# Cross-attention with a routed expert layer: eight expert tiles started from an early table

## The reference, cut to what matters

```
x = x + attention(context, context, layernorm(x))      # K, V from 120 context rows, one head, 8 batches
logits = layernorm(x) @ Wg + bg ; e = argmax(logits)   # one of 8 experts per row
h = gelu(layernorm(x) @ W1[e] + b1[e])
x = x + h @ W2[e] + b2[e]
```

## Time and profile before

| what | value |
|---|---|
| median of three runs | 483.49 us |
| profiled execution | 481.99 us, of which the span is 480.3 |
| PE busy, span | 409.1 us, 85% |
| DVE, ACT, POOL busy | 251.8, 203.5, 188.7 us |
| granted TensorE clock, mean | 0.936 of full |
| chain of waits, by engine | PE 66%, DMA 11%, issue 5%, DVE 5%, SP's queue 4% |

### The profile page before, as it was taken

The page is one execution under the profiler, slowest core; times in us unless marked ns, Lnnn a source line. Parts: engine busy times, 40 slices in busy tenths (PEclk is TensorE's granted clock), DMA queues, the critical chain, the costliest instruction groups (busy, mean ns, idle before and its releaser), DMA issues.

```text
span 480.3 us, 8534 instructions
## 1 busy us (share of the span) xinstructions
PE 409.1 (85%) x2050; PEld 223.8 (47%) x2051; DVE 251.8 (52%) x604; ACT 203.5 (42%) x411; POOL 188.7 (39%) x235
## 2 busy tenths in 40 slices
PE   6858999997998889997006899999999999999980
PEld 2355564565776666763002344444444444444430
DVE  0246899675466555676642345544544554454430
ACT  1132356646787666775232343224323323422310
POOL 7000001500034343543623465656566566656520
PEclk9969999999999988998557899999999999999997
DMA  7999975913535454458476999989888987999720
GB/s 252 322 323 382 379 288 195 385 48 112 197 113 162 145 175 134 143 165 306 150 248 153 166 177 197 177 189 213 191 193 212 192 196 183 224 191 191 150 46 0
DMA packets 116221, 94.46 MB, mean 197 GB/s; under 512 B 86744, under 2 KB 86756, under 8 KB 115943
## 3 DMA queue, kind: packets, MB, share of 16 engines
q1 hardware_dynamic: 108959, 74.68, 60.9%
q0 software_dynamic: 6400, 19.23, 11.1%
q10 hardware_dynamic: 840, 0.29, 0.3%
HBM read 54.50 MB, written 21.06 MB: 157 GB/s over the span
## 4 chain that ended last, share of the span: by engine, by line
PE 66%; DMA 11%; issue 5%; DVE 5%; SPq 4%; ACT 3%; POOL 2%; another core or an unknown queue 1%; ACTq 0%; DVEq 0%; POOLq 0%
PE bank L1292 24%; PE bank L1295 12%; DMA work<-in_ctx 5%; PE bank L1206 4%; PE bank L1226 4%; PE bank L1156 4%; PE bank L1244 4%; PE bank L1134 3%; PE bank L1219 3%; DMA key_bias_then_geluT<-work 3%; PE bank L1237 2%; PE bank L1116 1%; DMA expert_weights<-key_bias_split_then_xn 1%; ACT work L687 1%; SPq L450 1%
## 5 line engine op out<-in xcount | busy, mean ns | idle before, releaser
L1292 PE MATMUL bank<-expert_weights 128*128 x312 | 75.1, 384 | 22.2 <-DMA expert_weights<-key_bias_split_then_xn 20.8
L758 ACT ACTIVATE work<-work 128x512 f32<-128x512 f32 x39 | 24.6, 631 | 135.8 <-DVE work L1034 135.8
L589 POOL DMA_INDIRECT out_x<-work x39 | 45.3, 1162 | 87.2 <-DVE work L1050 85.0
L1292 PE MATMUL bank<-expert_weights,key_bias_then_geluT 128*128 x312 | 74.7, 383 | 4.5 <-DMA key_bias_then_geluT<-work 4.5
L1050 DVE SCALAR_TENSOR_TENSOR work<-bank,work 128x512 f32<-128x512 f32 x39 | 26.9, 691 | 75.4 <-PE bank L1295 75.4
L1292 PEld LDWEIGHTS bank<-expert_weights 128*128 128x128 f16 x312 | 30.9, 99 | 60.8 <-issue 26.9
L629 ACT ACTIVATE expert_weights<-expert_weights 128x512 f16<-128x512 f32 (+1 forms) x64 | 38.7, 626 | 38.2 <-DVE expert_weights L827 37.9
L1292 PEld LDWEIGHTS bank<-expert_weights,key_bias_then_geluT 128*128 128x128 f16 x312 | 30.7, 98 | 42.5 <-issue 7.7
L583 POOL TENSOR_TENSOR work<-work,values_then_b 128x512 f32<-128x512 f32 x39 | 49.2, 1261 | 0.2
L542 POOL DMA_INDIRECT routed_rows<-work,slot_index x32 | 32.4, 1012 | 37.2 <-DVE slot_index L921 29.9
L1034 DVE SCALAR_TENSOR_TENSOR work<-bank,keys_then_b 128x512 f32<-128x512 f32 x39 | 27.0, 692 | 35.3 <-PE bank L1295 21.5
(11 more groups left out here) (153 smaller groups left out, 608.5 us busy)
## 6 DMA issues: line engine op xcount, KB each, us to landing
expert_weights<-in_L_ffn_W SPq DMA_DIRECT2D x14, 1024.0 KB, 9.4
work<-routed_rows SPq DMA_DIRECT2D x39, 258.0 KB, 2.9
expert_weights<-in_x SPq DMA_DIRECT2D x16, 512.0 KB, 8.8
expert_weights<-in_x SPq DMA_DIRECT2D x32, 256.0 KB, 2.7
routed_rows<-values_then_b POOLq DMA_DIRECT2D x9, 258.0 KB, 9.2
expert_weights<-in_L_ffn_W SPq DMA_DIRECT2D x8, 256.0 KB, 3.0
keys_then_b<-in_L_ffn_b SPq DMA_DIRECT2D x1, 2048.0 KB
values_then_b<-in_L_ffn_b SPq DMA_DIRECT2D x1, 2048.0 KB, 9.5
```

Of the source, the lines that this page charges most:

```text
L589: pool.indirect_dma_start(out_rows, ids_of, rrow[t.buf][:, 0:D], None, bounds_check=T - 1, oob_is_err=False).then_inc(out_sent[t.buf], 16)
L1292: mm(o, a[:, c, :], w_split[:, bass.ds(first + (2 * c + h) * D, D)], start=(c == 0 and h == 0), stop=False)
```

## The change

- All high parts of experts 6 and 7 (16 of 64) move from ACT to POOL, two to four a group, after `scale` and before `route`. DVE's low parts of them are placed anew.
- Keys and values share one area `kv`. The last eight x tiles go into the part of it that is already used up (`xs2`, later the row buffers), so that expert 7 can be loaded a turn earlier.
- Once 5 of 8 groups (20 of 32 attention tiles) are placed, PE counts and DVE makes an early table of 8 (`NE`) full tiles. The late table holds the other 31, and subtracts the early ones (`early_q`).
- Expert tiles 0 to 7 run from the early table. Their first four are written between the last attention steps of each engine. Their biases come through PE: b1 and b2 are loaded early as 8 rows each, twice, split into high and low, and one matmul with a one-hot column adds the row to the product.
- b1 and b2 for tiles 8 to 38 are broadcast at SP's step 5, after it has waited for the late table and all routed rows.
- POOL waits once for the first output of every buffer before it sends tile 8. The hardware loop of the expert phase starts at tile 11 (`FIRST`).

SP, in the loop's head and in the expert steps:

```
             load_expert(E - 2, w_late)
-            with sp.Fori(1, NTURN) as i:
+            sp.wait_ge(bias_parts, 2)
+            for row in (0, LO_ROW):
+                for m, b in enumerate((b1, b2)):
+                    sp.dma_start(b_stage[row:row + E, D * m:D * (m + 1)], b).then_inc(b_in, 16)
+            with sp.Fori(1, NTURN - 1) as i:
...
+            def late_ready():
+                sp.wait_ge(tabled, 3)
+                for u in range(U):
+                    sp.wait_ge(sent[u], 16 * NTURN)
             def step(t):
                 if (t + 1).real:
                     transpose_x2(t + 1)
-                if (t + 4).real:
+                if isinstance(t.j, int) and t.j == NE - 3:
+                    late_ready()
+                    load_rows(t + 3, first_row((t + 3).j))
+                    sp.wait_ge(pv_done, NT)
+                    sp.dma_start(kv[:, b2_at:b2_at + E * D], b2.rearrange("e d -> (e d)").partition_broadcast(P))\
+                        .then_inc(b2_in, 16)
+                    sp.dma_start(b1_bc, b1.rearrange("e d -> (e d)").partition_broadcast(P)).then_inc(b1_in, 16)
+                if (t + 4).real and not (isinstance(t.j, int) and t.j == NE - 4):
                     load_rows(t + 4, first_row((t + 4).j))
                 if (t - 1).real:
                     transpose_g(t - 1)
```

POOL:

```
+            pool.wait_ge(b_in, 64)
+            for row in (0, LO_ROW):
+                nc.gpsimd.tensor_scalar(b_split[row:row + E, :], b_stage[row:row + E, :], WSCALE, 1.0, ALU.mult, ALU.mult)\
+                    .then_inc(b_high, 1)
+            highs_by_group = (2, 2, 2, 2, 4, 4)
+            for g in range(2 * NTURN - 2):
+                scale(seq, g, g % 2)
+                for _ in range(highs_by_group[g]):
+                    high(n_high)
+                    n_high += 1
+                if g >= 2:
+                    renumber(seq, g // 2 - 1, g % 2)
+                route(g, g % 2)
...
+            scale(seq, 2 * NTURN - 2, 0)
+            renumber(seq, NTURN - 2, 0)
+            pool.wait_ge(tx_done, NT)
+            xhat(Slot(0))
+            xhat(Slot(1))
+            step(Slot(0))
+            route(2 * NTURN - 2, 0)
+            step(Slot(1))
+            scale(seq, 2 * NTURN - 1, 1)
+            step(Slot(2))
+            renumber(seq, NTURN - 2, 1)
+            route(2 * NTURN - 1, 1)
```

ACT:

```
+            nc.scalar.activation(gelu_warm[:, :], half[:, 0:1], ACT.Gelu)
+            x2_high(Slot(0))
+            step(NT + 1, 1, NTURN)
+            x2_high(Slot(1))
+            x2_high(Slot(2))
+            gelu(Slot(0))
+            g_high(Slot(0))
+            step(NT + 2, 2, NTURN)
+            gelu(Slot(1))
+            g_high(Slot(1))
+            step(NT + 3, 3, NTURN)
+            x2_high(Slot(3))
```

DVE:

```
             for k in range(U):
                 step(seq, k, k, 0)
+                if k == 2:
+                    dve.wait_ge(b_high, 2)
+                    nc.vector.scalar_tensor_tensor(b_split[LO_ROW:LO_ROW + E, :], b_stage[LO_ROW:LO_ROW + E, :], WSCALE,
+                                                   b_split[LO_ROW:LO_ROW + E, :], ALU.mult, ALU.subtract)\
+                        .then_inc(b_low, 1)
...
+            lows = {0: 2, 2: 2, 4: 2, 6: 2}
+            for k in range(NT - U, NT + 1):
+                step(c, k, k % U, k // U)
+                for n in range(lows.get(k - NT + U, 0)):
+                    low(n_low)
+                    n_low += 1
+                if k == NT - U + 2:
+                    early_counts()
+                if k == NT - U + 3:
+                    early_table()
...
+            x2_low(Slot(0))
+            step(c, NT + 1, 1, NTURN)
+            x2_low(Slot(1))
+            x2_low(Slot(2))
+            g_low(Slot(0))
+            step(c, NT + 2, 2, NTURN)
+            g_low(Slot(1))
+            x2_low(Slot(3))
+            step(c, NT + 3, 3, NTURN)
+            g_low(Slot(2))
+            finish(Slot(0))
+            step(c, NT + 4, 4, NTURN)
+            step(c, NT + 5, 5, NTURN)
             nc.vector.engine_nop().then_inc(pairs_counted, 1)
+            x2_low(Slot(4))
             dve.wait_ge(counted, 1)
...
+            x2_low(Slot(5))
```

`early_counts` is 10 small chained operations (on 8 columns), `early_table` 8 (on 8 or 64 columns). PE:

```
+            def up(t, ex, hot=None):
+                if early(t):
+                    need(pe, g_done, t.j - 1)
+                    spread_row(bank[UP_BANK[t.half]][:, :], hot, 0)
+                    pe.wait_ge(x2T_in[t.half], 16 * t.pair + 16)
...
+            first4 = early_experts(0, C)
+            up_early(0, first4)
+            step(NT + 1, 1, NTURN)
+            up_early(1, first4)
+            step(NT + 2, 2, NTURN)
+            up_early(2, first4)
+            pe.wait_ge(x1_done, 2 * NT - 2)
+            down_early(0, first4)
+            step(NT + 4, 4, NTURN)
+            up_early(3, first4)
+            down_early(1, first4)
+            pe.wait_ge(pairs_counted, 1)
+            mm(bank[1][:, 0:E], ones_h[:, :], seen[:, 0, :], start=True, stop=True).then_inc(counted, 1)
+            last4 = early_experts(C, C)
+            pe.wait_ge(x1_done, 2 * NT)
+            for n in range(C, NE):
+                up_early(n, last4)
+                down_early(n - LAG, first4 if n - LAG < C else last4)
```

391 lines of the change are left out of this document (240 added, 151 removed).

## The result

The changed kernel takes 494.23 us (median of 4 runs, 493.16 to 496.71), the kernel before 485.03 (4 runs, 482.53 to 486.57): ratio 1.0201, 95% interval 1.0156 to 1.0246. It is slower, by 2.0%. The profiled execution's span is 491.5 us against 480.3.

The account below looks back on a forecast made before the run. TensorE's work was taken to set the pace around a 28 us hole. The ninth tile's start, 297.5 + 4.8 - 1.0 = 301.3 against 298.39, gave +2.9; with +0.5 late, net +3.4 us, forecast 486 us, range 470 to 495.

Parts of the forecast that it names:

- the sum: All terms together: net +3.4 us, point 486 us; that it holds as it stands, within 482 to 491, had 0.49.
- Part 4: Before tile 4's down product: its Gelu transpose queues behind 4 MB of bias broadcasts, a 7.5 us TensorE stall.
- the late part: Tiles 8 to 38: same work before and after; only POOL's one-time wait for the first outputs costs, +0.5 us.
- Part 1: Head of the attention: small bias loads land behind expert 6's 2 MB, delaying TensorE's transpose by 4.8 us.
- Part 2: Attention loop and last turn: high parts moved from ACT to POOL, -1.0 us, and rank(6) slipping, +1.2 us.
- Taken as hidden: Last attention turn: the early table's 18 small DVE operations, 4 us, cost nothing; up to 4 without cover.
- The high halves were said to free ScalarE, -1.0: Attention loop: 16 instructions of 0.626 us leave ACT for POOL, gaining 1.0 us (0 to 2).
- The slip of rank(6), +1.2: Last attention turn: POOL's scatters end later, so scale(6), the picks and group 6's rank slip 1.2 us (0 to 3).
- fourth case: Last turn: DVE and POOL exclude each other, lows 60 to 63 each waiting 0.76 us, 3.0 in all; 489.9, chance 0.07.
- Part 3: Early expert tiles: written order makes a serial chain with the attention's end; up 6 ends at 280.3 before earlier delays.
- The faster case: Neither bias load holds TensorE; small loads land early and transposes pass among the broadcast's packets: 473.3 us, chance 0.32.
- The slower case at 497.7: Early phase: a transpose takes 6.9 us instead of 3.3, three times waited for bare, 10.8 us; chance 0.12.

Follow-up runs that it names:

- Variant 1: Changed kernel with VectorE's wait for the bias rows and their subtraction moved from behind attention step 2 to behind step 7; 482.38 us, ratio 1.0226 to the kernel before.
- variant 4: Changed kernel with bias step behind step 7, attention steps 33 and 34 before the first early product, broadcasts in eight 512 KB pieces between transposes; 471.07 us, ratio 1.0027.
- variant 11: variant 4 with the early table one step later, b1's pieces first, residual sums of tiles 8 and 9 later; 477.14 us against 485.29, ratio 0.9817.
- variant 8: variant 4 with the late high halves back on ScalarE and the low halves spread on VectorE; 471.05 us, ratio 1.0007 to the kernel before.
- variant 3: Changed kernel with attention steps 33 and 34 ahead of the first early product on TensorE; 483.74 us, ratio 1.0243 to the kernel before.
- variant 2: Changed kernel with each late broadcast cut from eight bias rows to one, leaving out seven experts' biases in late tiles; 479.66 us, ratio 1.0181.
- variant 6: variant 4 with b1's pieces first and one piece behind each transpose of steps 5 to 8; 476.42 us, ratio 1.0118 to the kernel before.

## Why the prediction was right and wrong

The point was 486.0 and the likeliest class no change; 494.2 lies in the range (470 to 495), 0.8 us from its end, and the class is slower by over 1%, which had 0.29. That it lies in the range is luck of the chip: a range end of 495 is 1.024 of the 483.5 it started from, and on the second chip the change took 1.0411. The holes of Parts 1, 3 and 4 came where they were said. Of the 7.8 us that the sum lacks (+11.2 of span for +3.4), 0.1 had gathered by the end of up 6, 3.5 come in Part 4 and behind it, and 4.2 in the late part. The 0.1 is itself luck: on the first chip the attention began 1.26 us sooner, its last scores still came 4.8 us later than said (226.33 for 221.6, which is 217.78 plus 3.8), and the stretch from there to the last mix took 4.8 us less than said (25.65 for 30.4). Part by part, on the first chip's pair of profiles:

- **Part 1, +4.8: right in place, too small.** The loads landed at 126.06 (125.7 said), TensorE's transpose came at 130.59 (130.3 said). GpSimd took 2.15 us for 2.8, VectorE 1.22 for 0.8. What the term left out is the lower clock behind the gap, at which the next tile took 4.91 us instead of 2.88, and that the attention had started 1.26 us sooner. Variant 1 puts the whole at 7.1 us.
- **Part 2, +0.2: wrong, and the step that failed first.** "Taken as hidden: DVE works 16.8 of 30 us in the loop" read the mean load of a window at the loop's head, and the early table runs in the last turn, together with a group's picks and twice the low halves. There VectorE is busy over 9 us of 10 and takes its work in order, with the row maximum for ScalarE's exponential behind it:

```profile
134.00:204.00 70.00, 69.97 (x485) 50.87 (x483) 49.01 (x199) 58.68 (x148) 33.88 (x56) 1.00 0.55 167
204.00:214.00 10.00, 8.93 (x49) 5.41 (x48) 7.74 (x31) 6.54 (x19) 4.32 (x10) 0.91 0.80 241
```

```profile
134.00:204.00 70.00, 68.88 (x462) 48.93 (x461) 52.95 (x193) 52.97 (x136) 37.34 (x60) 1.00 0.58 182
204.00:214.00 10.00, 8.38 (x55) 5.54 (x56) 9.21 (x41) 4.73 (x12) 5.13 (x10) 1.00 0.28 85
```

  (before and after, second chip; VectorE is the third number with a count, ScalarE the fourth). VectorE's last steps of the table in variant 4, and the row maximum of the next tile right behind them, for which the transpose at 206.26 waits:

```profile
203.67 0.22 DVE L1115 TENSOR_TENSOR early_table_scratch<-tile_numbers,tiles_cumulated 128x64 f32<-128x64 f32 x1
...
205.10 0.17 DVE L1127 TENSOR_SCALAR early_tile_experts<-early_table_scratch 128x8 int32<-128x8 f32 x1
...
205.31 0.27 DVE L1032 TENSOR_REDUCE neg_row_max<-bank 128x1 f32<-128x120 f32 x1
```

  The attention stage grew by 9.8 us on the first chip and 13.9 on the second; less the 7.1 of Part 1 that leaves 2.7 and 6.8. On the second kind of chip variant 1 has it without Part 1's gap, 7.0 us longer than before (98.73 against 91.76): 1.1 are the bias step in its new place, 2.8 the three intervals behind tile 26 (11.74 against 3.18 + 2.88 + 2.89), at most 1.1 the meeting of GpSimd and VectorE. Of the 2.8 variant 11 shows 0.6 to 0.7 as the table's own; how the rest divides among the counts and the low halves was not tried. The last 2 us or so lie in small steps over many tiles; I lay them to VectorE's larger share (49.0 to 53.0 of 70), which is argued and not shown. The high halves were said to free ScalarE, -1.0: it was freed (58.7 to 53.0 us busy), but TensorE had no idle time there to win (69.97 of 70 busy in before). The slip of rank(6), +1.2: the scatters did end late, at 226.12 (223.7 said), since GpSimd stood 4.48 us for VectorE's low half ahead of its last highs, and `scale` followed at 226.19; but its squares were ready only 0.6 us sooner, so at most that much is the slip, and rank(6) came 3.26 us behind the last scores, where before has 4.47.
- **The rule on GpSimd and VectorE (fourth case).** In variant 4 the second of two high halves ends at 152.69 and the first at about 152.1, and VectorE's two-operand steps end at 152.15 and 152.73:

```profile
151.49 1.20 POOL L628 TENSOR_SCALAR expert_weights<-expert_weights 128x512 f16<-128x512 f32 x2
```

```profile
151.56 0.18 DVE L1004 TENSOR_REDUCE gate_max<-gate_logits_biased 128x4 f32<-128x32 f32 x1 [0.69 <-POOL gate_logits_biased L601]
151.78 0.37 DVE L1005 TENSOR_TENSOR gate_scratch<-gate_logits_biased,gate_max 128x32 f32<-128x32 f32 x1
152.18 0.55 DVE L1006 TENSOR_TENSOR gate_scratch<-gate_scratch,first_pick_rank 128x32 f32<-128x32 f32 x1
```

  The step with one operand is not held. By the Trainium skill, "SBUF — State Buffer", "Who interferes with whom", a VectorE instruction with two SBUF inputs contends with a GpSimd instruction that reads SBUF, and the shared ports are an exclusive lock. The trace agrees: each of the two such steps ends with a high half. It met the gate's small steps, not the low halves I had named, and costs at most 1.1 us (variant 8), not 3.
- **Part 3: nearly exact in its times, by errors that cancel.** With the +3.8 of the first parts it put the last mix at 252.0 (251.98 measured), rank(7) at 258.3 (258.95), up 3 at 259.0 (259.49), up 5 at 274.4 (275.09). But rank(6) came 2.3 us late (227.25 said, 229.59) and up 0 2 us (235.2 said, 237.16), and the chain from up 0 to the last mix then took 14.8 us for 16.8. The chain is serial as described: variant 3, with the attention's steps first, saves 7 us of it.
- **Part 4, 7.5: 9.8 measured.** TensorE wanted the transpose at 284.2 (280.3 plus 3.8 said), and from b2's issue to the transpose's end it took 15.2 us (14.4 said). The rest is that b2 was issued 1.6 us later than said. Another 1.2 us came behind it: down 4 took 5.0 us at the lower clock, for 4.1 said, and the two products behind it 5.9 for 5.6. The bytes are the cause, as variant 2 shows. The faster case, transposes that pass among the packets, did not come with whole broadcasts; once these were cut into pieces with the transposes between them (variant 4), 4 of the 10 us came back.
- **The late part, +0.5: 4.7 measured.** "Tiles 8 to 38 do the same work before and after" holds for the work and not for the waits. TensorE's gaps there are 3.8 us before and 7.4 after: 2.3 us more on Gelu transposes, 1.3 more of issue at the loop's turns; and 0.8 are the bias products of tiles 6 and 7. It came on two chips (4.7 and 3.6 us) and in all variants (170.6 to 175.0 where no stall fell into it). The lowest, 170.6, is variant 2's, whose waits for Gelu transposes (2.6 us) are those of the kernel before (2.6 and 2.8): the broadcasts' bytes may have a part in it, by one profile. Which of the moved buffers, the loop's later start or GpSimd's wait makes it, the runs do not tell.

The slower case at 497.7 gave nearly the right time by a mechanism that did not come: x2's transpose took 3.3 us from its issue to TensorE's start (233.88 to 237.16), as the sum has it, not 6.9.

## What to carry to other kernels

Before work is called hidden on an engine, read that engine's load in the very steps where it will run, and what stands behind it in its queue: mean load over a loop says nothing on a pile in its last turn. A wait taken into an in-order queue is priced with all that is queued behind it, and with the lower clock on TensorE after the gap; an idle time of 6.3 us cost 7.1. Large loads that are not urgent go in pieces between the urgent ones (4 of 10 us won here), but not so late that an in-order engine stands for the last piece (variant 6 gave back the 5 us that it had won, and more).

## What the hardware showed unexpectedly

- The same kernel differs by 3% between chips, and two kernels do not differ by the same factor: before 485 and 471 us, after 494 and 489. The change costs 2.0% on one kind and 4.1% on the other, and most of both lies in the attention (11 and 7 us).
- A transposing DMA behind 4 MB of broadcasts held the sync queue 8.75 us in its own issue, and 8.90 to 9.57 in three other profiles with whole broadcasts (1.2 to 1.6 for most others), so everything behind it in that queue waits as well: the next transpose was issued at 289.84.
- On the first kind of chip TensorE's granted clock fell to 0.66 between 174 and 184 us of the kernel before while it was busy 8.4 of 10 us, behind an idle time of 1.60 us at 176.55. In the same window variant 11, on a chip of that kind, has 0.83, and after on the first chip 1.00, with TensorE busy 8.5; on the second chip before has 1.00. The cause was not found.
